# Experts' step of a mixture-of-experts kernel: turns of the activations behind all gate and up products, down products and additions one step later

## What is computed

```python
logits = x @ router_w
top_val, top_idx = jax.lax.top_k(logits, K)            # K = 2
probs = jnp.zeros_like(logits).at[jnp.arange(T)[:, None], top_idx].set(jax.nn.sigmoid(top_val))
xin = probs.T[:, :, None] * x[None]
gu = jnp.einsum('etd,edf->etf', xin, gate_up_w)
gate, up = jnp.split(gu, 2, axis=-1)
h = jax.nn.silu(gate) * up
expert_out = jnp.einsum('eti,eid->etd', h, down_w)
combined = shared + expert_out.sum(axis=0)
```

## Time and profile before

| | us |
|---|---|
| median of 3 runs | 1229.82 |
| lowest and highest | 1227.98, 1230.69 |
| the profiled execution, its own time | 1228.41 |
| its span in the profile | 1226.7 |
| TensorE busy in the span | 1147.3 (94%) |
| first and last turn of the experts' stage (L1537) | 803.6, 1200.5 |

### The profile page before, as it was taken

The page is one execution under the profiler, slowest core; times in us unless marked ns, Lnnn a source line. Parts: engine busy times, 40 slices in busy tenths (PEclk is TensorE's granted clock), DMA queues, the critical chain, the costliest instruction groups (busy, mean ns, idle before and its releaser), DMA issues. The chain is left out here.

```text
span 1226.7 us, 21498 instructions
## 1 busy us (share of the span) xinstructions
PE 1147.3 (94%) x5638; PEld 704.4 (57%) x5639; DVE 745.8 (61%) x1254; ACT 510.1 (42%) x936; POOL 783.2 (64%) x524
## 2 busy tenths in 40 slices
PE   6999999999999999999987999829999999999994
PEld 2445545555545555455437999726666666666662
DVE  6677776776777777767714754365555554555553
ACT  2456666666666666656644222151111111111110
POOL 1597887977878878778880077534555555555553
PEclk8799999999999999999987999959999999999997
DMA  6668667677676686775524996423455555667771
GB/s 181 176 166 211 189 181 214 179 193 206 182 211 184 175 218 186 186 205 158 150 73 168 366 374 233 140 72 116 157 159 172 179 190 187 206 201 217 217 239 65
DMA packets 116301, 229.49 MB, mean 187 GB/s; under 512 B 19038, under 2 KB 21854, under 8 KB 116256
## 3 DMA queue, kind: packets, MB, share of 16 engines
q1 hardware_dynamic: 84496, 159.30, 43.9%
q0 software_dynamic: 23632, 54.19, 14.9%
q10 hardware_dynamic: 8128, 15.47, 3.9%
HBM read 149.35 MB, written 97.86 MB: 202 GB/s over the span
## 5 line engine op out<-in xcount | busy, mean ns | idle before, releaser
L769 DVE TENSOR_REDUCE row_max<-bank 128x1 f32<-128x512 f32 x512 | 342.3, 686 | 152.8 <-PE bank L588 150.4
L701 ACT ACTIVATE probsT<-bank 128x512 f32<-128x512 f32 x512 | 299.9, 597 | 200.2 <-PE bank L600 196.9
L457 POOL TENSOR_TENSOR key_sum<-key_sum,probsT 128x1024 f32<-128x1024 f32 x128 | 299.9, 2372 | 0.0
L588 PE MATMUL bank<-k_stack,q_stack 96*128 96x512 f32 x512 | 278.9, 548 | 6.7 <-DVE row_max L769 2.8
L453 POOL TENSOR_TENSOR key_sum<-probsT 128x1024 f32<-128x1024 f32 x64 | 151.4, 2376 | 111.2 <-ACT probsT L701 111.2
L600 PE MATMUL bank<-q_stack,k_stack 99*128 99x512 f32 x512 | 207.9, 407 | 1.6 <-ACT probsT L701 1.5
L588 PEld LDWEIGHTS bank<-k_stack,q_stack 96*128 96x128 f32 x512 | 98.4, 193 | 166.4 <-DVE row_max L769 127.8
L1499 ACT ACTIVATE gated<-bank,slot_info 128x256 f32<-128x256 f32 x71 | 33.7, 474 | 322.0 <-PE bank L1556 322.0
L1549 PE MATMUL bank<-gate_up_hi,rows_hi 128*128 x284 | 136.3, 480 | 15.2 <-issue 14.4
L1575 PE MATMUL bank<-down_sb,act_hT 128*128 x284 | 139.1, 612 | 7.7 <-issue 4.6
L1396 POOL DMA_INDIRECT out<-partner_rows,slot_info x71 | 72.8, 1026 | 111.4 <-DVE partner_rows L1462 110.6
(11 more groups left out here) (145 smaller groups left out, 1701.0 us busy)
## 6 DMA issues: line engine op xcount, KB each, us to landing
expert_rows_dram<-zero_rows SPq DMA_DIRECT2D x16, 1152.0 KB, 7.2
expert_rows_dram<-rows_out SPq DMA_DIRECT2D x71, 256.0 KB, 3.1
k_stack<-hi_dram SPq DMA_DIRECT2D x60, 256.0 KB, 6.6
q_stack<-hi_dram SPq DMA_DIRECT2D x60, 256.0 KB, 7.1
x_row<-in_x SPq DMA_DIRECT2D x16, 512.0 KB, 3.9
rows_ext_dram<-hid SPq DMA_DIRECT2D x16, 512.0 KB, 5.6
hidT_dram<-hidT SPq DMA_DIRECT2D x16, 512.0 KB, 2.9
tok<-hidT_dram SPq DMA_DIRECT2D x16, 512.0 KB, 7.4
```

Source lines behind the costliest of these rows:

```text
L457: nc.gpsimd.tensor_tensor(total, total, probs(k), ALU.add).then_inc(added, 1)
L588: nc.tensor.matmul(logit_bank[i % 2][:, :], q_stack[par][g][0:K_LOGIT, h, q * P:(q + 1) * P], k_stack[par][g][0:K_LOGIT, h, :], start=True ...
L701: nc.scalar.activation(probsT[:, j, :], key_bank[j % 2][:, :], ACT.Exp, scale=SCALE).then_inc(probs_ready, 1)
L769: nc.vector.tensor_reduce(row_max[g][:, i:i + 1], logit_bank[i % 2][:, :], AX.X, ALU.max)\
```

## The change

On PE `turn_h(n - 1)` leaves `gate_up(n)` and stands behind its last product. `down` in step n is that of tile n - 2 and no longer that of tile n - 1; it stays the last piece of the step, behind `turn_in(n + 1)`. On DVE `add_rest` and `add_partner` in step n are those of tiles n - 2 and n - 3. On POOL `gather_partners` and `scatter` in step n are those of tiles n - 2 and n - 3; `gather(n + 2)` stays where it is in its step. The loops of DVE and POOL have one step more. `DEPTH`, `AHEAD`, all buffers, all waits in the functions and the streams of ACT and SP stay as they are.

```diff
--- before.py
+++ after.py
@@ -1403,13 +1403,13 @@
                 for n in range(PARTNERS):
                     nc.gpsimd.memset(partner_rows[n][:, :], 0.0).then_inc(partner_cleared, 1)
                 pool.wait_ge(partner_cleared, PARTNERS)
-                for n in range(NT + 2):
+                for n in range(NT + 3):
                     if n + AHEAD < NT:
                         gather(n + AHEAD)
-                    if 0 <= n - 1 < NT:
-                        gather_partners(n - 1)
-                    if 0 <= n - 2:
-                        scatter(n - 2)
+                    if 0 <= n - 2 < NT:
+                        gather_partners(n - 2)
+                    if 0 <= n - 3:
+                        scatter(n - 3)
                 for i in range(PARTNERS):
                     pool.wait_ge(final_scattered[i], 16 * tiles_in(i, PARTNERS))
 
@@ -1466,17 +1466,17 @@
                     lower_weights(c)
                 lower_in(0)
                 dve.wait_ge(partner_cleared, PARTNERS)
-                for n in range(NT + 2):
+                for n in range(NT + 3):
                     if 0 <= n - 1 < NT:
                         copy_h(n - 1)
                     if n < NT:
                         combine(n)
                     if n + 1 < NT:
                         lower_in(n + 1)
-                    if 0 <= n - 1 < NT:
-                        add_rest(n - 1)
-                    if 0 <= n - 2:
-                        add_partner(n - 2)
+                    if 0 <= n - 2 < NT:
+                        add_rest(n - 2)
+                    if 0 <= n - 3:
+                        add_partner(n - 3)
 
             @block3.scalar
             def _(act):
@@ -1548,8 +1548,6 @@
                             w = part[:, bass.ds(e * KT + k, 1), :].rearrange("p o f -> p (o f)")
                             nc.tensor.matmul(gu_bank[i % 2][:, :], rows_hi[i % 2][:, k, :], w,
                                              start=(k == 0 and part is gate_up_hi), stop=False)
-                    if exists(n - 1):
-                        turn_h(n - 1, i - 1)
                     pe.wait_ge(in_lo_ready, n + 1)
                     for k in range(KT):
                         w = gate_up_hi[:, bass.ds(e * KT + k, 1), :].rearrange("p o f -> p (o f)")
@@ -1579,12 +1577,12 @@
                 def step(n, i, m):
                     if exists(n):
                         gate_up(n, i, expert(n))
-                    elif exists(n - 1):
+                    if exists(n - 1):
                         turn_h(n - 1, i - 1)
                     if exists(n + 1):
                         turn_in(n + 1, i + 1, m + (i + 1) // DEPTH)
-                    if exists(n - 1):
-                        down(n - 1, i - 1, expert(n - 1))
+                    if exists(n - 2):
+                        down(n - 2, i - 2, expert(n - 2))
                 turn_in(0, 0, 0)
                 pe.wait_ge(weights_hi_ready, CHUNKS)
                 pe.wait_ge(weights_lo_ready, CHUNKS)
```

## The result

| | us |
|---|---|
| before, median of 4 runs beside the change | 1229.07 |
| changed, median of 4 runs (1522.52 to 1524.75) | 1523.53 |
| ratio, with its 95% interval | 1.2394 (1.2376 to 1.2411) |
| span of the profiled execution, before and changed | 1226.7 and 1520.8 |

The forecast was 1480 with a range of 1405 to 1520: the direction and the mechanism came as told, the time fell 3.5 us beyond the range. In the profile after, the lines of the changed kernel have moved by two: the products with `rows_lo` are L1554, the turns of `act_h` L1563, the down products L1573.

What follows compares the result with a forecast made beforehand. TensorE was taken to set the pace. The ring's 8.30 us plus 0.84 for the clock gave steps of 9.14 against 5.47: 242 us over 66 steps, plus 8 at the ends, made 1480 us, range 1405 to 1520.

Steps and rivals of the forecast that it cites:

- TensorE's own work: TensorE's matmuls and turns in a step of the experts' stage, without waits: 5.14 us, unchanged by the new order.
- the pause: TensorE's idle time ahead of the turn of `rows_in` in each step, waiting for the gather: 3.16 us.
- the ring: Turn, down products, `add_rest`, gather, next turn, each waiting for the one before: 8.30 us a step against 5.47.
- the turn's place: Turn of `act_h` moved behind the gate and up products on TensorE: gain taken as 0, at most 22.9 us.
- 0.96 us of cover: Time from the end of `copy_h` (904.22) to the start of the down products that wait for it (905.18).
- The ends: Tile 4's later turn, 2 us, and the work behind the last turn, 6 us, added outside the steps.
- The clock: TensorE's clock falling to half around the wait: 0.4 of steps at 2.1 us, 0.84 us a step.
- all steps slow: Rival: every step of the experts' stage at half clock, step 10.4 us, time 1563 us; chance 0.07.
- A clock that holds: Rival: TensorE stays at full clock through its waits, step 8.30 us, time 1425 us; chance 0.21.
- The shorter ring: Rival: the gather lands in 3.4 to 4.0 us and the clock holds, 1355 to 1395 us; chance 0.06.
- The faster case: Rival: the gather ahead of the turn of `rows_in` stays hidden, landing under 1.62 us, time 1207 us; chance 0.02.

Runs made afterwards that it cites:

- e5: The kernel before with only the turn of `act_h` moved behind the gate and up products: 1241.01 us, ratio 1.0086.
- e1: The changed kernel with the turn of `act_h` put back in the middle of the products: 1527.13 us, ratio 1.2414 to the kernel before.
- e4: The changed kernel with 18 idle products of 256 columns ahead of each turn's wait: 1442.38 us, ratio 1.1716 to the kernel before.
- e9: The changed kernel with 12 idle products of 256 columns ahead of each turn's wait: 1440.58 us, ratio 1.1684 to the kernel before.
- e8: The changed kernel with the down products ahead of the turn on TensorE and `add_rest` ahead of `lower_in` on DVE: 1285.02 us, ratio 1.0437 to the kernel before.

## Why the prediction was wrong, point by point

**The bound and TensorE's own work.** Right but for the pause. The old order had no waits to win. The pause that is left of the ring was put at 3.16 us and measured 2.4: from the start of the turn at 958.52 to the end of the turn of `act_h` at 964.37 (963.99 and its 0.38) TensorE takes 5.85 us of the ring, not 5.14. The gain of the turn's place was taken as 0 with bounds of 22.9 us of gain and nothing of loss; e5 shows that it costs 10 us when moved alone. The loss was left out, though the working had the number for it, 0.96 us of cover. In the whole change it plays no part, as e1 shows.

**The ring.** Right in each link, and the decisive step of the forecast. It was put at 8.30 us and measured 8.52 in e4 and 8.43 in the eight steps of the changed kernel at full clock. In the two steps shown the turn to the down products took 0.87 and 1.01 us; the landing took 4.5 in the median instead of 4.45, with a little for the hand over at either end. By the ring of e4 this makes 0.22 x 66 = 15 us of the miss.

**The ends.** Put at 8 us. The turn of tile 4 came at 840.65, 1.2 us later than before (839.43) although the stage's first product had come 0.5 us earlier, so 1.7 us; from the last turn to the end it took 32.5 instead of 26.1 us. Together 8.

**The clock.** This is the step that failed. Its working held that a slow step costs 2.1 us, that a slow step leaves no pause, that falls therefore work against the next, and took 0.4 of the steps as slow: 0.84 us a step. Measured were 58 of 66, 0.88, and 1.48 us each (10.00 - 8.52), in all 9.81 - 8.52 = 1.29 us a step. The term was 0.84 x 66 = 55 and is 85 us, 30 us more; with the 15 of the ring this is the miss of 44 us. e9 gives the same size without counting, 83 us. The argument went wrong in one point: it let a slow step run wholly at the half clock. In the trace the half clock that began at 967.4 was over before 971. By then the down products were through, and of the gate and up products behind them most often only the first started at half clock, five of them at most, so that a slow step still ended in a pause (over all steps TensorE stood still for 158.1 / 66 = 2.4 us ahead of the turn) and the clock fell again. The half clock was granted in only 30% of the stage, but in the part that lies on the ring. That a slow step costs 1.48 and not 2.1 has the same cause: the fall came behind the turn's start, often with the turn and the first of the down products through at full clock.

**The range.** Its upper end was a step of 9.74 us, with two thirds of the steps slow. The working itself named all steps slow as a bound at 10.4 and gave it 0.07. The measured step, 9.81, lies between; the range was cut inside a bound that I had no row to exclude.

**The rivals.** A clock that holds would have given 1425; e9 and e4 made that kernel, 1440 to 1442, the difference being the 15 us of the ring. The shorter ring did not come: the landing went from 4.3 to 4.5 us, not down. The mean traffic of the stage did fall, from 190 to 106 GB/s, but not beside the gathers: the ring puts nearly all transfers of a step into the same 4.5 us. Here is the changed kernel while no gather is under way and from a gather's start to its turn, and behind them the gather of the earlier trace rows in the kernel before:

```profile
958.52:962.36 3.84, 3.63 (x14) 2.22 (x14) 1.65 (x3) 0.60 (x1) 0.00 (x0) 1.00 0.00 1
962.36:966.89 4.53, 2.01 (x10) 1.41 (x8) 1.24 (x3) 0.47 (x1) 3.01 (x3) 1.00 0.61 189
...
905.20:909.50 4.30, 4.30 (x16) 2.90 (x17) 2.69 (x5) 0.61 (x2) 2.16 (x3) 1.00 0.55 169
```

What a gather would take with little beside it is shown by no run here. The faster case needed a landing of 1.62 us; the smallest was 4.2. The rule of the Trainium skill (page "TensorE: Matmul & The Clock Gate", section "Loop structure matters more than you think") that matmuls with a long DMA wait ahead of each run cold stood nearer to the truth than my 0.4: the trace agrees for the down products, in 58 of 66 steps, and not for most of the gate and up products behind them, which ran at full clock. The figure of the Trainium skill, page "DMA: Bandwidth & Descriptors" (section "Anatomy of one DMA — SWDGE (gpsimd) path"), an estimate of 3.2 us for such a gather, is not borne out by 4.2 to 5.1.

## What to carry to other kernels

When a consumer of a buffer is moved by a step, follow the buffer and not the consumer: write down what its refill waits for and who waits for the refill, and add up the links. If a link stands behind the very instruction that waits, the sum is the step time, however busy the engines were, and one more buffer may be worth more than a better order: here 4 KB a partition brought 1523.5 us to 1236.2, and e8's order with the old buffers only to 1285.0. Where the ring leaves TensorE a pause, look at which work comes first behind it: here that work lay on the ring, and a half clock for 30% of the time made the step 1.29 us longer, 15%.

## What the runs showed that I had not expected

A pause of 2.0 us in the mean, repeated each 10 us, brought the clock down as surely as one of 2.4 (57 and 58 falls), 1.5 us in some half of the steps (36), 1.1 us hardly ever (2). The forecast had put its pause at 3.2 us and given falls to 0.4 of the steps. Products that compute nothing paid for themselves: 12 of them a step took 83 us off the kernel. The ring bunches the transfers: the stage moved 106 GB/s in the mean instead of 190, and still 189 GB/s beside a gather, which did not land sooner. And the last 0.4% that a fifth buffer seemed to bring was one DRAIN at the end, of 1.8 instead of 9.1 us.
